# Moving layer 1's first layer norm and its first two turns into the last steps of layer 0's attention

## The chip, the cores and the metric

The kernel runs on one core of a Trainium2 chip. The metric is the device time of one execution in microseconds; 870.31 us is the median of three runs of the kernel before (868.54, 870.31 and 872.8). The profile is of another execution of the same kernel. TensorE (PE) does the matmuls and the transposes, VectorE (DVE), ScalarE (ACT) and GpSimd (POOL) the rest, and SyncE (SP) issues most DMAs. Each engine works through its own list of instructions in order; they are tied together by semaphores that count up.

## The reference, cut to what matters

Sixteen sequences of 256 tokens with 128 features pass two layers. Each layer normalises, and adds to x an attention and a mixture of experts of the normalised x.

```
xn = layernorm(x)                                    # (x - mean) / sqrt(var + 1e-5), by token
x  = x + softmax_attention_16_heads(xn) + top2_experts(xn)      # layer 0
xn = layernorm(x)                                    # the first step of layer 1
q, k, v = xn @ Wq, xn @ Wk, xn @ Wv;  gated = xn @ W1;  logits = xn @ Wr
x  = x + retention(q, k, v, gated) + top_p_experts(xn, logits)  # layer 1
```

The change is about the place where layer 0's attention of the last sequences ends and layer 1's projections begin. Layer 1's layer norm of a sequence can start when that sequence's x is complete: attention added, experts added.

## The kernel before, in words

Layer 0's attention works in 64 groups of four heads: group g belongs to sequence g // 4. All engines run through slots n = 0 to 67 (`run_groups`, with TAIL0 = 4 slots behind the last group). The order in each slot is written out by hand, as a function `slot` for each engine, and spreads a group over several slots. PE in slot n: the early scores of group n+3, in slots with n % 4 = 2 the turn of a finished sequence's heads (`turn_heads`), in slots with n % 4 = 3 its output projection (`attention_out`), the transposed scores of group n (`scores_t`), the turn of group n-2's output (`turn_out`), the late scores of n+3, the turn of the row maxima of n+2 (`turn_max`), and the weighting of the values of group n-1 (`weigh`). ACT: the copy of the turned heads in slots with n % 4 = 2 (`put_heads0`), the exponential of group n (L808), the negation of the row maxima of n+2 (`negate_max`, L782), the evacuation of n-1 (`evacuate`, L788). DVE: the second row maximum of n+2 (`row_max_second`, L1163), in slots with n % 4 = 3 the addition of a sequence's attention (`add_attention`, L1244), the division of n-2 (`divide`, L1234 and L1236), the first row maximum of n+3 (L1158), and statistics for layer 1's norm (`stats_of`). SP moves the negated maxima into the query stack (L464), from where `scores_t` two slots later reads them. POOL masks the exponentials of group n.

A sequence's attention is added four slots after its last group; the last sequence, 15, ends as slot 66 (turn of heads), slot 67 (output projection, addition, statistics).

Layer 1's norm takes the variances in two lots, EARLY for the first 24 tiles of 128 tokens (sequences 0 to 11) and LATE for the other eight. `variance_of(EARLY)` stands in DVE's slot 60, behind `divide` and the first row maximum. Behind all slots come, on ACT, the square root (`deviation1`, with a load of the function table), then, when `shift_of` on DVE has given reciprocal and shift, `normalise(0,0)`, `normalise(1,1)`, `high_x(0,0)`, `normalise(2,0)`, `high_x(1,1)`. `normalise` takes a sequence in two activations (L851) and `high_x` copies its turned form out of PSUM (L856); `low_x` on DVE (L1279) makes the rest for the two-part fp32 products. PE waits for all of layer 0's additions, then `transposes(0,0)` and `transposes(1,1)` (L1690), then for each of the sixteen sequences `products` (twelve matmuls, L1696) and `transposes` of the sequence two further on. This is what stands at PE's seam:

```
            run_groups(slot, middle, TAIL0)
            pe.wait_ge(x_attn, B)
...
            pe.wait_ge(consts_ready, 7)
            transposes(0, 0)
            transposes(1, 1)
```

PSUM banks 0 and 1, which take the turns, hold scores in layer 0; bank 7 and the upper half of bank 6 hold layer 0's turned output and heads, and later the second sequence's second product.

Of the kernel before, what the change touches and what calls it, by code (L numbers as in the profile page):

```python
# [13 lines left out]
ds = bass.ds  # L14
# [46 lines left out]
def build(nc, a, out):  # L61
    ctx = ExitStack()
    with ctx:
# [218 lines left out]
        def run_groups(slot, middle=None, tail=0):  # L282

            for n in range(G0 + tail):
                if n == MIDDLE * RING and middle is not None:
                    middle()
                slot((0, n))
# [77 lines left out]
        def ps_t1(u): return ps[:, u, 0:S]  # L365
# [373 lines left out]
        def _(act):  # L739
# [44 lines left out]
            def evacuate(g):  # L784
                act.wait_ge(pv_done, num(g) + 1)
                if past(g, 2):
                    act.wait_ge(o_turned, num(g) - 1)
                nc.scalar.activation(o_ring[:, at(g, 2), :], ps_o, ACT.Copy).then_inc(o_evac, 1)  # L788
# [12 lines left out]
            def slot(g):  # L801
                if g[1] % GPB0 == 2 and past(g, 6):
                    put_heads0(div(plus(g, -6), GPB0), 1 - g[1] // GPB0 % 2)
                if within(g, G0):
                    act.wait_ge(st_done, num(g) + 1)
                    if past(g, 2):
                        act.wait_ge(pv_done, num(g) - 1)
                    nc.scalar.activation(probs[:, at(g, 2), :, :], ps[:, 3:6, :], ACT.Exp, scale=float(D) ** -0.5)\  # L808
                      .then_inc(exp_done, 1)
                if within(plus(g, 2), G0):  # L810
                    negate_max(plus(g, 2))
                if past(g, 1) and within(plus(g, -1), G0):
                    evacuate(plus(g, -1))
                if num(g) == COUNT + 1:
                    act.wait_ge(pick_d, 1)
                    nc.scalar.activation(r_s[:, 1, 0, :], r_s[:, 0, 0, :], ACT.Exp).then_inc(pick_e, 1)
# [15 lines left out]
            def put_down(e):  # L832
# [1 line left out]
                for c in range(2 * e, 2 * e + 2):  # L834
                    last = nc.scalar.activation(y_sb[:, c, :], ps[:, 4 + e % 2, (c - 2 * e) * D:(c - 2 * e + 1) * D], ACT.Copy, scale=p_slot[:, c:c + 1])
                last.then_inc(y_put, 1)
            run_groups(slot, middle, TAIL0)

            def deviation1(n, tiles):
                act.wait_ge(var_ready, n)  # L840
                nc.scalar.activation(std[:, tiles], var[:, tiles], ACT.Sqrt).then_inc(std_ready, 1)
            deviation1(1, EARLY)


            def normalise(b, u):

# [7 lines left out]
            def high_x(b, v):  # L854
                act.wait_ge(tr_done, B + b + 1)
                nc.scalar.activation(r32(x_hl[:, 0, ds(b * S, S)]), ps_t1(v % 2), ACT.Copy).then_inc(xh_put, 1)  # L856

            def parts(b, v):
                u = v % 2
                act.wait_ge(p1_mm, b + 1 + CREDIT)  # L860
                nc.scalar.activation(sg[:, ds(b * TB, TB), :], p1_both(u)[:, :, D + E:PROJ1], ACT.Silu).then_inc(sg_put, 1)
                if isinstance(b, int) and b == 3:
                    deviation1(2, LATE)
                if more(b, 2):
                    high_x(b + 2, (v + 2) % 4)
                if more(b, 3):
                    act.wait_ge(tr_done, B + b + 2)
                    normalise(b + 3, 1 - u)
            act.wait_ge(rstd_ready, 2 * B + 2)
            act.wait_ge(wo_mm, B)  # L870
            normalise(0, 0)
            normalise(1, 1)
            high_x(0, 0)
            normalise(2, 0)
            high_x(1, 1)

            def step1(b, v):
                parts(b, v)
# [92 lines left out]
        def _(dve):  # L971
# [212 lines left out]
            def slot(g):  # L1184
                n = num(g)
                if within(plus(g, 2), G0) and n != MIDDLE * RING:
                    row_max_second(plus(g, 2))
                if n == COUNT:
                    take_counts()
                if n == FIND + 1:  # L1190
                    index_out()
                if n % GPB0 == 3 and n >= 7:
                    add_attention(div(plus(g, -7), GPB0))
                if n >= 2 and within(plus(g, -2), G0):
                    divide(plus(g, -2))
                if within(plus(g, 3), G0):
                    row_max_first(plus(g, 3))
                if n == 0:
                    add_router_bias()
                    mark_best(0)  # L1200
                if n == 1:
                    pick_first(0)
                if n == 2:
                    mark_best(1)
                if n == 3:
                    pick_first(1)
                if n == COUNT + 1:
                    count_ahead()
                if n == COUNT + 2:
                    pick_places()  # L1210
                if n == COUNT + 3:
                    index_in()
                if n == COUNT + 4:
                    mark_tiles()
                    weigh_experts()
                for m in range(MARKS):
                    if MARK - 1 + m * (FIND - MARK + 1) // MARKS == n:
                        mark_rows(m)
                for b in range(B):
                    if pair_counted(b) == n:  # L1220
                        stats_of(b)
                if n == G0 - 4:
                    variance_of(EARLY)
                if n == G0 + 3:
                    variance_of(LATE)

            def divide(g):

# [37 lines left out]
            run_groups(slot, middle, TAIL0)  # L1266


            def shift_of(n, tiles):
                dve.wait_ge(std_ready, B + n)  # L1270
                nc.vector.reciprocal(rstd[:, tiles], std[:, tiles]).then_inc(rstd_ready, 1)
                dve.wait_ge(rstd_ready, 2 * B + 2 * n - 1)
                nc.vector.scalar_tensor_tensor(out=shift[:, tiles], in0=moments[:, tiles, 0], scalar=-1.0, in1=rstd[:, tiles],
                                               op0=ALU.mult, op1=ALU.mult).then_inc(rstd_ready, 1)
            shift_of(1, EARLY)

            def low_x(b, v):
                dve.wait_ge(xh_put, b + 1)
                nc.vector.tensor_tensor(r32(x_hl[:, 1, ds(b * S, S)]), ps_t1(v % 2), x_hl[:, 0, ds(b * S, S)], ALU.subtract).then_inc(xl_put, 1)  # L1279
            dve.wait_ge(wo_mm, B)  # L1280
            low_x(0, 0)
            low_x(1, 1)
            dve.wait_ge(late_in, 13 * 16)

            def parts(b, v):
# [164 lines left out]
        def _(pe):  # L1450
# [137 lines left out]
            def slot(g):  # L1588
# [23 lines left out]
                    find_slots()  # L1612
                if past(g, 1) and within(plus(g, -1), G0):
                    weigh(plus(g, -1))

            def find_slots():

                pe.wait_ge(rows_marked, MARKS)
                pe.wait_ge(tiles_known, 10)
                for n in range(2 * NT):  # L1620
                    last = nc.tensor.matmul(ps_slots, of_row[:, n, :], of_tile[:, n, :, :].rearrange("p u c -> p (u c)"),
                                            start=(n == 0), stop=(n == 2 * NT - 1), skip_group_check=True)
                last.then_inc(slots_mm, 1)
# [56 lines left out]
                    down(e)  # L1680
                pe.wait_ge(y_put, E)
            run_groups(slot, middle, TAIL0)
            pe.wait_ge(x_attn, B)


            def transposes(b, u):
                pe.wait_ge(xn_second, (b + 1) * TB)
                pe.wait_ge(xl_put, b + 1)
                for t in range(TB):
                    last = nc.tensor.transpose(ps_t1(u)[:, t * P:(t + 1) * P], xn1_ring[:, u, t, :], ident[:, :])  # L1690
                last.then_inc(tr_done, 1)

            def three(dst, lhs, rhs):

                for k, (i, j) in enumerate(((0, 0), (1, 0), (0, 1))):
                    last = nc.tensor.matmul(dst, r32(lhs[i]), r32(rhs[j]), start=(k == 0), stop=(k == 2))  # L1696
                return last

            def products(b, v):
                u = v % 2  # L1700
                pe.wait_ge(xl_put, b + 1 + CREDIT)
                rhs = [x_hl[:, i, b * S:(b + 1) * S] for i in range(2)]
                pe.wait_ge(qk1_put, b + 1)
                for c in range(2):
                    last = three(ps_qk1(u)[:, c * S:(c + 1) * S], [w[:, c * P:(c + 1) * P] for w in w1_qk], rhs)
                last.then_inc(qk1_mm, 1)
                pe.wait_ge(lg1_put, b + 1)
                for t in range(TB):
                    last = three(ps_p1(u, t), [x_[:, t * P:(t + 1) * P] for x_ in rhs], [w[:, :] for w in w1_p])
                last.then_inc(p1_mm, 1)  # L1710
            pe.wait_ge(consts_ready, 7)
            transposes(0, 0)
            transposes(1, 1)

            def step(b, v):
                products(b, v)
# [225 lines left out]
```

## Time and profile before

| what | value |
|---|---|
| median of three runs | 870.31 us (868.54 to 872.8) |
| the profiled execution's own time | 864.98 us |
| its span, first to last instruction | 863.2 us |
| mean granted TensorE clock | 0.944 of full |
| PE busy | 755.5 us, 88% of the span |
| DVE, ACT, POOL busy | 556.3, 421.7, 311.3 us |
| share of PE in the chain that ended last | 70% |

Busy time is the union of an engine's instructions. The chain that ended last is followed back from the last instruction, at each step to what released it. Slot 61 begins at about 353.5 us of the span and the first products of layer 1 start at 376.01 us.

### The profile page before, as it was taken

How to read it: one execution, taken by the hardware profiler on the slowest of the kernel's cores; microseconds unless marked ns; L12 is line 12 of the kernel's file. 1: busy time of each engine (PE TensorE's matmuls, PEld its weight loads, DVE VectorE, ACT ScalarE, POOL GpSimd, SP SyncE). 2: the span in 40 equal slices, each digit the busy share in tenths (PEclk: the TensorE clock that was granted, in tenths of full speed). 3: DMA queues.
4: the chain of work that ended last, by engine and by line, in shares of the span. 5: the costliest groups of instructions: out<-in, count | busy, mean ns of one | idle time of the engine just before them, and what ended most of it. 6: DMA issues, size and time to landing. Idle time of an engine off the chain costs nothing.

```text
span 863.2 us, 17725 instructions
## 1 busy us (share of the span) xinstructions
PE 755.5 (88%) x6148; PEld 587.6 (68%) x6148; DVE 556.3 (64%) x1076; ACT 421.7 (49%) x788; POOL 311.3 (36%) x399
## 2 busy tenths in 40 slices
PE   4757889967978999768698879999999999999997
PEld 3644556745845666558576668888888888888886
DVE  4956799633534677547698757665656566666665
ACT  4723455534433656567666634444444444444442
POOL 1742357532032577500377736221211212121211
PEclk9977899988978999979899979999999999999999
DMA  5763465322012464100021137121111121211100
GB/s 174 223 198 118 134 196 201 93 73 79 8 53 74 133 180 134 51 2 1 27 64 51 50 92 147 39 67 42 61 48 61 49 61 49 61 49 61 49 13 12
DMA packets 58130, 70.71 MB, mean 82 GB/s; under 512 B 6608, under 2 KB 37840, under 8 KB 58064
## 3 DMA queue, kind: packets, MB, share of 16 engines
q1 hardware_dynamic: 56320, 67.46, 26.7%
q0 software_dynamic: 1024, 2.10, 0.8%
q8 instruction: 41, 0.67, 0.3%
q10 hardware_dynamic: 720, 0.27, 0.1%
q14 instruction: 25, 0.20, 0.1%
HBM read 53.80 MB, written 15.86 MB: 81 GB/s over the span
## 4 chain that ended last, share of the span: by engine, by line
PE 70%; DVE 10%; issue 6%; DMA 4%; ACT 3%; another core or an unknown queue 2%; POOL 2%; SPq 2%; ACTq 0%; DVEq 0%; POOLq 0%
PE ps L1696 23%; PE ps L1849 20%; PE ps L1562 3%; PE ps L1737 3%; PE ps L1545 3%; PE ps L1510 2%; DVE m L1163 2%; DMA q_st<-m_neg 2%; PE ps L1493 2%; PE ps L1663 1%; PE ps L1542 1%; PE ps L1628 1%; PE ps L1568 1%; PE ps L1497 1%
## 5 line engine op out<-in xcount | busy, mean ns | idle before, releaser
L1381 DVE SCALAR_TENSOR_TENSOR f_l<-ps,f_h 128x512 fp32r<-128x512 f32 x256 | 176.0, 691 | 114.1 <-ACT f_h L891 112.9
L891 ACT ACTIVATE f_h<-ps 128x512 fp32r<-128x512 f32 x256 | 153.3, 600 | 196.7 <-PE ps L1696 196.7
L1696 PE MATMUL ps<-x_hl,w_h 128*128 (+1 forms) x512 | 201.3, 393 | 0.0
L724 POOL TENSOR_TENSOR acc<-acc,yt 128x512 f32<-128x512 f32 x55 | 71.0, 1291 | 249.8 <-DVE yt L1419 249.8
L808 ACT ACTIVATE probs<-ps 128x1536 f32<-128x1536 f32 x64 | 92.9, 1452 | 78.6 <-PE ps L1545 71.0
L1696 PEld LDWEIGHTS ps<-x_hl,w_h 128*128 128x128 f32 x512 | 96.7, 189 | 19.7
L1849 PE MATMUL ps<-f_l,w_h 128*128 128x512 f32 x256 | 99.7, 390 | 0.6 <-DVE f_l L1381 0.6
L1696 PE MATMUL ps<-x_hl,w_l 128*128 (+1 forms) x256 | 100.1, 391 | 0.0
L1849 PE MATMUL ps<-f_h,w_h 128*128 128x512 f32 x256 | 99.7, 390 | 0.0
L1849 PE MATMUL ps<-f_h,w_l 128*128 128x512 f32 x256 | 99.6, 389 | 0.0
L633 POOL TENSOR_SCALAR_AFFINE_SELECT probs<-probs 128x512 f32<-128x512 f32 x96 | 63.6, 686 | 98.0 <-ACT probs L808 97.7
L1163 DVE TENSOR_REDUCE m<-ps 128x4 f32<-128x1024 f32 x64 | 77.8, 1216 | 5.0 <-PE ps L1510 4.8
L1234 DVE RECIPROCAL rden<-ps 128x8 f32<-128x8 f32 x64 | 13.2, 206 | 83.5 <-PE ps L1628 62.4
L1849 PEld LDWEIGHTS ps<-f_l,w_h 128*128 128x128 f32 x256 | 48.1, 188 | 11.1 <-DVE f_l L1381 1.1
L1696 PEld LDWEIGHTS ps<-x_hl,w_l 128*128 128x128 f32 x256 | 48.4, 189 | 9.5
L1849 PEld LDWEIGHTS ps<-f_h,w_l 128*128 128x128 f32 x256 | 48.1, 188 | 10.0
L1849 PEld LDWEIGHTS ps<-f_h,w_h 128*128 128x128 f32 x256 | 48.1, 188 | 10.0
L1562 PE MATMUL ps<-probs,v_ring 128*16 128x256 f32 x512 | 43.4, 413 | 8.2 <-DVE wv_tok L1236 8.2
L1158 DVE TENSOR_REDUCE m<-ps 128x4 f32<-128x512 f32 x64 | 43.6, 681 | 6.0 <-PE ps L1497 6.0
L788 ACT ACTIVATE o_ring<-ps 128x256 f32<-128x256 f32 x64 | 24.6, 385 | 43.5 <-PE ps L1568 26.4
L1330 DVE TENSOR_TENSOR sc<-ps,upto 128x1024 f32<-128x1024 f32 x32 | 37.8, 1219 | 8.5 <-PE ps L1737 7.8
L1510 PE MATMUL ps<-k_st,q_st 72*128 72x256 bf16 x256 | 42.7, 293 | 0.0
(226 smaller groups left out, 1427.3 us busy)
## 6 DMA issues: line engine op xcount, KB each, us to landing
gate_b<-gate_rows SPq DMA_DIRECT2D x64, 256.0 KB, 3.3
k_st<-qk_parts SPq DMA_DIRECT2D x32, 288.0 KB
q_st<-qk_parts SPq DMA_DIRECT2D x96, 96.0 KB
qk_parts<-qk_p SPq DMA_DIRECT2D x16, 384.0 KB, 2.8
y_tok<-zero SPq DMA_DIRECT2D x8, 512.0 KB, 3.3
w_raw<-in_w_e SPq DMA_DIRECT2D x16, 256.0 KB, 2.8
x_rows<-xn_ring SPq DMA_DIRECT2D x16, 128.0 KB, 2.6
w_up<-in_w_up SPq DMA_DIRECT2D x8, 256.0 KB, 2.9
```

Of the source, the lines that this page charges most:

```text
L633: nc.gpsimd.affine_select(tiles, tiles, pattern=[[0, GH], [1, P]], compare_op=ALU.is_ge, fill=0.0, base=0, channel_multiplier=-1)\
L724: nc.gpsimd.tensor_tensor(acc[:, :], acc[:, :], yt[:, e % 2, :], ALU.add).then_inc(summed, 1)
L808: nc.scalar.activation(probs[:, at(g, 2), :, :], ps[:, 3:6, :], ACT.Exp, scale=float(D) ** -0.5)\
L891: nc.scalar.activation(r32(f_h[:, m % 4, :]), ps[:, m % 4, :], ACT.Relu).then_inc(f_hi, 1)
L1158: nc.vector.tensor_reduce(m8[:, at(g, 2), :, 0], ps[:, first, :].rearrange("p (h k) -> p h k", h=GH), AX.X, ALU.max).then_inc(early_max, 1)
L1163: nc.vector.tensor_reduce(m8[:, at(g, 2), :, 1], ps[:, first + 1:first + 3, :].rearrange("p c (h k) -> p (c h) k", h=2), AX.X, ALU.max).th ...
L1330: nc.vector.tensor_tensor(sc[:, i % 3, :, 0:2 * P].rearrange("p h (j t) -> p h j t", t=P), diagonal(i % 2), upto[:, :].unsqueeze(1).unsque ...
L1381: nc.vector.scalar_tensor_tensor(out=r32(f_l[:, m % 4, :]), in0=ps[:, m % 4, :], scalar=0.0, in1=f_h[:, m % 4, :], op0=ALU.max, op1=ALU.su ...
L1510: last = nc.tensor.matmul(dst(1 + h // 2)[:, h % 2 * S:(h % 2 + 1) * S], qs[0:R0, h, P:S], ks[0:R0, h, :], start=False, stop=True, skip_gr ...
L1562: nc.tensor.matmul(ps_o[32 * h:32 * h + 2 * HD0, :], v_ring[:, u, 0, k * GH + h, :], probs[:, at(g, 2), 1 + h // 2, h % 2 * S:(h % 2 + 1) ...
L1696: last = nc.tensor.matmul(dst, r32(lhs[i]), r32(rhs[j]), start=(k == 0), stop=(k == 2))
L1849: last = nc.tensor.matmul(ps[:, 4 + e % 2, :], r32(w[i]), r32(fs[:, m % 4, :]), start=(c == 0 and k == 0), stop=(c == FC - 1 and k == 2))
```

## The change

In the slots of all three engines new steps are put in for the last groups (G0 is 64). EARLY's variances move from DVE's slot 60 to slot 62. The square root goes into ACT's slot 63, reciprocal and shift into DVE's slot 64, `normalise(0,0)` into ACT's slot 64, the first turn into PE's slot 65, and `normalise(1,1)`, `high_x(0,0)`, `normalise(2,0)`, `high_x(1,1)` into ACT's slot 66; `low_x(0,0)` into DVE's slot 66, `low_x(1,1)` into slot 67, the second turn into PE's slot 66. The waits in front of layer 1 on ACT (`wo_mm`), DVE (`wo_mm`) and PE (`x_attn`) go; PE's comes back ahead of the second sequence's second product, and PE gets three waits for the banks that the first steps take over. The bodies of the moved functions are otherwise the same.

```diff
@@ ScalarE, slot
+                if num(g) == G0 - 1:
+                    deviation1(1, EARLY)
+                if num(g) == G0:
+                    act.wait_ge(rstd_ready, 2 * B + 2)
+                    normalise(0, 0)
+                if num(g) == G0 + 2:
+                    normalise(1, 1)
+                    high_x(0, 0)
+                    normalise(2, 0)
+                    high_x(1, 1)
@@ ScalarE, behind the slots
-            deviation1(1, EARLY)
...
-            act.wait_ge(rstd_ready, 2 * B + 2)
-            act.wait_ge(wo_mm, B)
-            normalise(0, 0)
-            normalise(1, 1)
-            high_x(0, 0)
-            normalise(2, 0)
-            high_x(1, 1)
@@ VectorE, slot
-                if n == G0 - 4:
+                if n == G0 - 2:
                     variance_of(EARLY)
+                if n == G0:
+                    shift_of(1, EARLY)
+                if n == G0 + 2:
+                    low_x(0, 0)
                 if n == G0 + 3:
                     variance_of(LATE)
+                    low_x(1, 1)
@@ VectorE, behind the slots
-            shift_of(1, EARLY)
...
-            dve.wait_ge(wo_mm, B)
-            low_x(0, 0)
-            low_x(1, 1)
@@ TensorE, slot
+                if num(g) == G0 + 1:
+                    pe.wait_ge(max_done, G0)
+                    transposes(0, 0)
+                if num(g) == G0 + 2:
+                    transposes(1, 1)
+                if num(g) == G0 + 3:
+                    pe.wait_ge(consts_ready, 7)
+                    pe.wait_ge(exp_done, G0)
@@ TensorE, products
                 pe.wait_ge(lg1_put, b + 1)
+                if b == 1:
+                    pe.wait_ge(x_attn, B)
@@ TensorE, behind the slots
-            pe.wait_ge(x_attn, B)
...
-            pe.wait_ge(consts_ready, 7)
-            transposes(0, 0)
-            transposes(1, 1)
```

## Rows read from the trace of the kernel before

**Rows 1.** Chain that ended last, 340 to 400 us: start, duration, what.
```profile
342.91 0.56 PE ps L1562 x8
...
343.68 0.32 PE ps L1493
344.00 0.23 PE ps L1497 x4
...
345.38 0.22 PE ps L1628 x2
...
353.54 1.60 DVE moments L1173 x24
...
356.99 0.97 PE ps L1562 x8
...
360.29 0.42 PE ps L1628 x2
...
376.01 2.97 PE ps L1696 x12
...
383.58 1.46 PE ps L1696 x12
```

**Rows 2.** Timeline of DVE, slots 60 and 61: start, duration, operation, idle before.
```profile
353.45 1.68 DVE L1173 BATCH_NORM_AGGREGATE moments<-stats 128x2 f32<-128x6 f32 x24
...
355.25 1.22 DVE L1163 TENSOR_REDUCE m<-ps 128x4 f32<-128x1024 f32 x1
```

**Rows 3.** Timeline of PE, slot 61 to the first turns of layer 1.
```profile
356.53 0.27 PE L1524 MATMUL ps<-ident,m 128*8 128x128 f32 x1 [1.96 <-DVE m L1163]
...
361.34 0.62 PE L1562 MATMUL ps<-probs,v_ring 128*16 128x256 f32 x8 [0.65 <-DVE wv_tok L1236]
...
368.13 0.44 PE L1628 MATMUL ps<-ident,o_ring 128*128 128x128 f32 x2 [0.50 <-ACT o_ring L788]
369.17 0.41 PE L1636 MATMUL ps<-ident,wv_tok 128*128 128x128 f32 x2 [0.61 <-issue]
370.14 0.68 PE L1642 MATMUL ps<-w_o,wvn 128*128 128x128 f32 x4 [0.56 <-ACT wvn L794]
374.35 1.26 PE L1690 MATMUL ps<-ident,xn_ring 128*128 128x128 f32 x4 [3.52 <-ACT xn_ring L851]
```

**Rows 4.** Timeline of ACT, slot 61 to the first normalised sequences.
```profile
354.39 1.45 ACT L808 ACTIVATE probs<-ps 128x1536 f32<-128x1536 f32 x1 [0.35 <-PE ps L1545]
...
365.26 0.39 ACT L788 ACTIVATE o_ring<-ps 128x256 f32<-128x256 f32 x1 [0.28 <-PE ps L1568]
367.69 0.39 ACT L788 ACTIVATE o_ring<-ps 128x256 f32<-128x256 f32 x1 [2.04 <-PE ps L1568]
369.62 0.39 ACT L794 ACTIVATE wvn<-ps 128x256 f32<-128x256 f32 x1 [1.54 <-PE ps L1636]
370.02 1.28 ACT L841 ACT_TABLE_LOAD   x1
371.31 0.22 ACT L841 ACTIVATE std<-var 128x24 f32<-128x24 f32 x1
373.22 1.66 ACT L851 ACTIVATE xn_ring<-x,shift,rstd 128x128 f32<-128x128 f32 x4 [1.68 <-DVE shift L1273]
375.05 0.39 ACT L856 ACTIVATE x_hl<-ps 128x256 fp32r<-128x256 f32 x1 [0.17 <-PE ps L1690]
```

**Rows 5.** Timeline of DVE, shift and first rest of layer 1.
```profile
372.67 0.29 DVE L1271 RECIPROCAL rstd<-std 128x24 f32<-128x24 f32 x1
...
375.53 0.42 DVE L1279 TENSOR_TENSOR x_hl<-ps,x_hl 128x256 fp32r<-128x256 f32 x1 [2.35 <-ACT x_hl L856]
```

**Rows 6.** Chain that ended last over the whole span: one move of row maxima.
```profile
329.12 2.43 DMA q_st<-m_neg
```

**Rows 7.** Stretches of 1 us: busy us (count) by engine, granted clock, DMA share, GB/s.
```profile
357.00:358.00 1.00, 1.00 (x16) 0.54 (x16) 0.00 (x0) 0.10 (x1) 0.13 (x1) 0.56 0.08 16
...
381.00:382.00 1.00, 1.00 (x10) 1.00 (x10) 0.42 (x1) 0.34 (x2) 0.00 (x0) 0.99 0.08 16
```

More of the change, by code:

```diff
@@ L836, in put_down @@
                 last.then_inc(y_put, 1)
-            run_groups(slot, middle, TAIL0)
             def deviation1(n, tiles):
@@ L856, in high_x @@
                 nc.scalar.activation(r32(x_hl[:, 0, ds(b * S, S)]), ps_t1(v % 2), ACT.Copy).then_inc(xh_put, 1)
+            run_groups(slot, middle, TAIL0)
             def parts(b, v):
@@ L1221, in slot, with shift_of, low_x @@
                         stats_of(b)
-                if n == G0 - 4:
+                if n == G0 - 2:
                     variance_of(EARLY)
+                if n == G0:
+                    shift_of(1, EARLY)
+                if n == G0 + 2:
+                    low_x(0, 0)
                 if n == G0 + 3:
                     variance_of(LATE)
+                    low_x(1, 1)
+            def shift_of(n, tiles):
+                dve.wait_ge(std_ready, B + n)
+                nc.vector.reciprocal(rstd[:, tiles], std[:, tiles]).then_inc(rstd_ready, 1)
+                dve.wait_ge(rstd_ready, 2 * B + 2 * n - 1)
+                nc.vector.scalar_tensor_tensor(out=shift[:, tiles], in0=moments[:, tiles, 0], scalar=-1.0, in1=rstd[:, tiles],
+                                               op0=ALU.mult, op1=ALU.mult).then_inc(rstd_ready, 1)
+            def low_x(b, v):
+                dve.wait_ge(xh_put, b + 1)
+                nc.vector.tensor_tensor(r32(x_hl[:, 1, ds(b * S, S)]), ps_t1(v % 2), x_hl[:, 0, ds(b * S, S)], ALU.subtract).then_inc(xl_put, 1)
             def divide(g):
@@ L1266, in _ @@
             run_groups(slot, middle, TAIL0)
[L1269 to L1274, printed above, removed]
-            shift_of(1, EARLY)
-            def low_x(b, v):
-                dve.wait_ge(xh_put, b + 1)
-                nc.vector.tensor_tensor(r32(x_hl[:, 1, ds(b * S, S)]), ps_t1(v % 2), x_hl[:, 0, ds(b * S, S)], ALU.subtract).then_inc(xl_put, 1)
-            dve.wait_ge(wo_mm, B)
-            low_x(0, 0)
-            low_x(1, 1)
             dve.wait_ge(late_in, 13 * 16)
@@ L1614, in slot, with transposes, three, products @@
                     weigh(plus(g, -1))
+                if num(g) == G0 + 1:
[6 more added lines that the diff above has]
+                    pe.wait_ge(exp_done, G0)
+            def transposes(b, u):
+                pe.wait_ge(xn_second, (b + 1) * TB)
+                pe.wait_ge(xl_put, b + 1)
+                for t in range(TB):
+                    last = nc.tensor.transpose(ps_t1(u)[:, t * P:(t + 1) * P], xn1_ring[:, u, t, :], ident[:, :])
+                last.then_inc(tr_done, 1)
+            def three(dst, lhs, rhs):
+                for k, (i, j) in enumerate(((0, 0), (1, 0), (0, 1))):
+                    last = nc.tensor.matmul(dst, r32(lhs[i]), r32(rhs[j]), start=(k == 0), stop=(k == 2))
+                return last
+            def products(b, v):
+                u = v % 2
+                pe.wait_ge(xl_put, b + 1 + CREDIT)
+                rhs = [x_hl[:, i, b * S:(b + 1) * S] for i in range(2)]
+                pe.wait_ge(qk1_put, b + 1)
+                for c in range(2):
+                    last = three(ps_qk1(u)[:, c * S:(c + 1) * S], [w[:, c * P:(c + 1) * P] for w in w1_qk], rhs)
+                last.then_inc(qk1_mm, 1)
+                pe.wait_ge(lg1_put, b + 1)
+                if b == 1:
+                    pe.wait_ge(x_attn, B)
+                for t in range(TB):
+                    last = three(ps_p1(u, t), [x_[:, t * P:(t + 1) * P] for x_ in rhs], [w[:, :] for w in w1_p])
+                last.then_inc(p1_mm, 1)
             def find_slots():
@@ L1682, in _ @@
             run_groups(slot, middle, TAIL0)
-            pe.wait_ge(x_attn, B)
[L1686 to L1710, printed above, removed]
-            pe.wait_ge(consts_ready, 7)
-            transposes(0, 0)
-            transposes(1, 1)
             def step(b, v):
```

## The prediction

> **What bounds the kernel now.** I read the chain that ended last first, cut to 340 to 400 us, the stretch of the change. PE holds it nearly everywhere; the reader is to see the pieces that are not PE. One is DVE's aggregation for EARLY, 1.60 us of the chain at 353.54 [rows 1]. Then the timelines of single engines give the reason. In slot 60 DVE takes the 24 aggregations and one small operation from 353.45 to 355.25, 1.80 us, and only then the last group's second row maximum [rows 2]; PE, which has nothing left but to turn these maxima, idles 1.96 us for it [rows 3]. The second hole is at the seam: after the last output projection (370.14) PE does nothing for 3.52 us until ACT has normalised [rows 3]; ACT loads a table (1.28 us) and takes a root (0.22) from 370.02, waits 1.68 for DVE's shift, and needs 0.83 for each sequence [rows 4]. Last, the granted clock in stretches of 1 us: it falls from full to half between 357 and 358 us, just after the first hole, and the first products of layer 1 run at half as well, to 381 us [rows 7]: the first twelve matmuls take 2.97 us, twelve later ones 1.46 [rows 1]. So both holes are on the path that sets the end, and each is followed by half-clock work. From 383 us on the projections are a train of matmuls, so what is gained ahead of them is kept.
>
> All sums are against the profiled execution, 864.98 us (span 863.2 and 1.8 around it). That is 5.3 us below the median of the three runs, 870.31; I subtract the gain from that median, since nothing ties the difference to the stretch of the change.
>
> **Part 1, the variances go from slot 60 to slot 62.** Removed ahead of the row maximum: 355.25 - 353.45 = 1.80 us [rows 2]. The maximum then ends at 353.45 + 1.22 = 354.67, PE turns it at once, and with the division behind it on DVE (about 0.45) the weighting of group 60 starts near 355.15 instead of 356.99: 1.84 earlier. That closes the 1.96 us hole to some 0.3, and I expect no fall of the clock there. From that weighting to the end of the turn that feeds the next division there are six PE groups: 356.99 to 360.29 + 0.42, 3.72 us at half clock. The same six a few slots earlier take 342.91 to 345.38 + 0.22, 2.69, less 0.32 + 0.23 for two score groups that the last slots no longer have: 2.14 [rows 1]. Difference 1.58. What is late next: the turn of sequence 14's heads also waits for the negated maxima, which stand on ACT behind group 61's exponential, 354.39 + 1.45 = 355.84 [rows 4], and 0.27 more: 356.1, where the shortened work would be there at 355.9. That costs 0.2. Sum: 1.84 + 1.58 - 0.2 = **3.2 us**; the weighting of group 61 starts at 358.1, not 361.34 [rows 3]. If the clock falls all the same, the 1.58 goes and 1.6 is left; that is the low end.
>
> The negated maxima go through SP's queue; a move took 2.43 us from its issue to its landing where the chain ran through one [rows 6], so the last lands at 356.1 + 2.45 = 358.6, and the scores that read it come behind a weighting and an output projection, near 359.4. Covered by 0.8. SP has nothing ahead of it in these slots, and layer 1's first loads, next in its queue, come earlier too.
>
> The 1.80 us of variances now stand in slot 62 behind the division and ahead of the addition of sequence 14. Until DVE's next division is due PE must weight group 61 (0.62 and as much again), project (0.68) [rows 3], do group 63's scores (about 0.7) and turn (0.4): some 2.8 us against 1.80 + 0.42 for the addition. Cost nothing; with no such cover it would be the whole 1.80, the high end of its cost.
>
> **Part 2, the seam**, reckoned on the clock times of before and then shifted by part 1. ACT's copy of group 62's output ends at 365.65; load and root, 1.50, end at 367.15, and group 63's copy is not due before 367.69 [rows 4]. So 1.50 us of ACT are hidden, 0.54 to spare. DVE's reciprocal and shift, 372.67 to 373.2, 0.5 us [rows 4, 5], are then done at 367.7, while DVE is free.
>
> Here the Trainium skill, "ScalarE: Activation LUTs", section "What ACT_TABLE_LOAD costs", speaks against the change: a switch costs the load of about 1283 ns and a drain of about 1380 ns, 2.66 us in all. The trace agrees on the load and shows no drain: it starts 0.01 us after the copy ahead of it and the root 0.01 after it [rows 4]. By the page, group 63's copy would be 0.8 us late and the sum below 5.7 instead of 6.5.
>
> The steps from there: group 63's copy ends at 368.08; `normalise(0,0)`, half of 1.66, to 368.9; PE starts some 0.25 after its release, so the first turn runs 369.2 to 369.65. Behind it the turn of heads is late: 369.65 instead of 369.17, to 370.05 [rows 3]. ACT copies it (0.39) to 370.5, then `normalise(1,1)` to 371.35. PE's second turn waits for that, 371.6 to 372.05, and the last output projection, which was at 370.14, queues behind the turn: 372.05 to 372.65. So the added wait costs sequence 15's attention about 1.9 us; who waits for it is DVE's addition, and through it only the second sequence's second product. The first products need the rest of x: `high_x(0,0)` (0.39) to 371.75, `low_x(0,0)` (0.42) [rows 4, 5] to 372.2, earlier than PE is free. They start at 372.7, not 376.01 [rows 1]: **3.3 us**. Next in line is `low_x(1,1)`, behind addition, statistics and LATE's variances on DVE: 372.65 + 0.42 + 0.5 + 0.8 + 0.42, 374.9. With the first products at half clock (372.7 + 2.97 + turn = 376.1) it is hidden; at full clock PE would be there at 374.5 and wait 0.4 to 0.5.
>
> **The clock behind it** is the cost that no row gives. From group 62's weighting to the first products PE has about 8.3 us with short groups, busy some half of them, and the trace shows a fall of the clock after just such work. Low end of the gain: it falls ahead of the seam; then five short PE groups take 0.2 us more each, 1.0 in all. High end: it stays full, the first two products give back 1.5 each, less the 0.5 of waiting and another 1.0 of ACT and DVE that fall in behind, so 1.5. I take nothing, nearest to before, where two sequences' products ran at half.
>
> Sum: 3.2 + 3.3 = 6.5 us; 870.31 - 6.5 = **863.8 us** (the profiled execution 858.5).
>
> **The cases.**
> *Forecast, 863.8 us, chance 0.47*: both holes shorten, clock low for part of the time as before; its own range 862.5 to 865.5.
> *Clock stays full through the seam, 862.3 us, 0.20*: 6.5 + 1.5 = 8.0. For it: the two holes before the falls are nearly gone. Against: PE stays half idle for 8 us.
> *The first gain is small, 866.4 us, 0.22*: the clock still falls near 357 us (1.6 left of 3.2) and falls ahead of the seam (3.3 - 1.0), 3.9 in all. For it: what ended the stay at full clock was not the one hole alone; PE had been waiting off and on before the second fall. Against: PE is nearly dense up to 358 us now.
> *The change does not do what it says, 869 us, 0.06*: the waits only move. PE's turns block the last projection, ACT's load makes group 63 late, and the seam gives 0 to 1 us in place of 3.3, while part 1 gives its 1.6 less the variances' 1.80 showing up in slot 62. Against: the covers of 0.54, 0.8 and 0.6 us worked out above.
> *Slower, 876 us, 0.05*: the clock stays at half in the projections. Each sequence costs 2.97 - 1.46 = 1.5 us more at half [rows 1]. It decides from the fifth additional sequence on (5 x 1.5 = 7.5 against 6.5); with eight it is 12.0 - 6.5 = 5.5 slower. For it: the products start after a longer sparse stretch without a dense one. Against: in the trace a dense run brings the clock back, at 381 us, five after its start [rows 7].
>
> A measurement of this kernel can tell about 0.5%, 4.35 us, from no change: faster means below 865.96. That holds all of the first two cases but a twentieth, and a third of the third: 0.73; same 0.22; slower 0.05. The range of 8 in 10 runs from 860.6 to 867.4: it takes in the full clock, most of the third case, and the spread of 4 us among the runs of before.
>
> **What would show it.** In the changed kernel's trace: the wait of PE's turn of the maxima (L1524, its last) at 0.1 us or so, not 1.96; a granted clock of 1.00 from 354 to 360; no gap on DVE's side of more than 0.1 us ahead of group 62's weighting; the table load directly behind the second-last copy of outputs, and the last copy not later after its weighting than 0.1 us; PE's first products 6.5 us earlier, at 369.5, directly behind the last output projection; the second sequence's products not waiting more than 0.5. It is wrong if the table load shows a tail, if the last scores wait for the move of the maxima, if PE waits for DVE's division in slot 63, or if the clock stays at half beyond the third sequence.

## The result and the profile after

Six runs of the changed kernel gave 859.18 us in the median (855.65 to 860.35), six of the kernel before 870.09 (867.76 to 873.77): ratio 0.9869, interval 0.9836 to 0.9902, which is 11.4 us faster (8.5 to 14.3); the two medians differ by 10.9. I had forecast 863.8 with a range from 860.6: right in direction, too small in size, and outside the range by 1.4 us. The profiled execution took 856.11 us, 8.9 less than the one of before, with a span of 853.1, 10.1 less.

From the page of the changed kernel: span, busy PE, and the granted clock in 40 slices of the span (9 is 0.9 or more).

```profile
span 853.1 us, 17724 instructions
...
PE 754.8 (88%) x6148; PEld 585.8 (69%) x6148; DVE 556.3 (65%) x1076; ACT 420.5 (49%) x788; POOL 311.1 (36%) x399
...
PEclk9977899988978999999799879999999999999999
```

PE does the same work in the same busy time. What changed is where it stood still. The timeline of PE in the changed kernel, from the last turn of maxima to the first products (start, duration, operation, idle before); it answers to [rows 3]:

```profile
354.24 0.27 PE L1528 MATMUL ps<-ident,m 128*8 128x128 f32 x1
354.74 0.62 PE L1566 MATMUL ps<-probs,v_ring 128*16 128x256 f32 x8 [0.23 <-DVE wv_tok L1253]
...
357.53 0.62 PE L1566 MATMUL ps<-probs,v_ring 128*16 128x256 f32 x8 [0.65 <-DVE wv_tok L1253]
...
359.51 0.38 PE L1667 MATMUL ps<-ident,o_ring 128*128 128x128 f32 x2
360.55 0.63 PE L1566 MATMUL ps<-probs,v_ring 128*16 128x256 f32 x8 [0.65 <-DVE wv_tok L1253]
...
364.31 0.44 PE L1667 MATMUL ps<-ident,o_ring 128*128 128x128 f32 x2 [0.49 <-ACT o_ring L788]
365.12 0.41 PE L1632 MATMUL ps<-ident,xn_ring 128*128 128x128 f32 x2 [0.37 <-issue]
365.37 0.40 PE L1675 MATMUL ps<-ident,wv_tok 128*128 128x128 f32 x2
367.00 0.44 PE L1632 MATMUL ps<-ident,xn_ring 128*128 128x128 f32 x2 [1.24 <-ACT xn_ring L857]
367.27 0.61 PE L1681 MATMUL ps<-w_o,wvn 128*128 128x128 f32 x4
367.93 0.36 PE L1638 MATMUL ps<-x_hl,w_qk_hi 128*128 128x256 f32 x1
```

The idle 1.96 us ahead of the turn of maxima is gone, and of the 3.52 us in front of layer 1 there is left 1.24 in front of the second turn. The first products start at 367.93, not 376.01 [rows 1].

ACT in the changed kernel, slots 63 to 66, as [rows 4]:

```profile
361.45 0.38 ACT L788 ACTIVATE o_ring<-ps 128x256 f32<-128x256 f32 x1 [0.28 <-PE ps L1572]
361.85 1.28 ACT L849 ACT_TABLE_LOAD   x1
363.14 0.22 ACT L849 ACTIVATE std<-var 128x24 f32<-128x24 f32 x1
363.87 0.38 ACT L788 ACTIVATE o_ring<-ps 128x256 f32<-128x256 f32 x1 [0.51 <-PE ps L1572]
364.15 0.87 ACT L857 ACTIVATE xn_ring<-x,shift,rstd 128x128 f32<-128x128 f32 x2
365.80 0.38 ACT L794 ACTIVATE wvn<-ps 128x256 f32<-128x256 f32 x1 [0.78 <-PE ps L1675]
366.08 0.86 ACT L857 ACTIVATE xn_ring<-x,shift,rstd 128x128 f32<-128x128 f32 x2
```

The table load and the root stand in ACT's wait for group 63; 0.51 us of that wait is left over, where 0.54 had been reckoned. There is no tail behind the load: the root starts 1.29 us after the load does, as before.

DVE in the changed kernel, as [rows 2, 5]:

```profile
352.98 1.21 DVE L1164 TENSOR_REDUCE m<-ps 128x4 f32<-128x1024 f32 x1
...
357.30 1.68 DVE L1174 BATCH_NORM_AGGREGATE moments<-stats 128x2 f32<-128x6 f32 x24
...
359.38 0.41 DVE L1261 TENSOR_TENSOR x<-x,ps 128x256 f32<-128x256 f32 x1
359.93 0.21 DVE L1251 RECIPROCAL rden<-ps 128x8 f32<-128x8 f32 x1
...
369.72 0.42 DVE L1242 TENSOR_TENSOR x_hl<-ps,x_hl 128x256 fp32r<-128x256 f32 x1
```

The variances now run from 357.30, and with the addition behind them DVE is busy to 359.79. PE's turn, which the next division waits for, ends at 359.51 + 0.38 = 359.89. So they are hidden, but by 0.1 us, where the prediction had about 0.6: the steps on PE took 2.36 us, not 2.8.

The clock, in stretches of 6 us of the changed kernel (busy us and count by engine, granted clock, DMA share, GB/s), against the falls of [rows 7]:

```profile
356.00:362.00 6.00, 4.21 (x57) 2.87 (x55) 3.23 (x30) 4.23 (x7) 2.64 (x6) 1.00 0.66 173
362.00:368.00 6.00, 3.21 (x31) 1.90 (x31) 2.24 (x10) 4.70 (x12) 0.45 (x1) 1.00 0.01 4
368.00:374.00 6.00, 5.62 (x45) 5.33 (x46) 5.22 (x21) 4.79 (x12) 0.00 (x0) 1.00 0.02 4
```

It is full all the way, though PE is busy only half of the middle stretch.

### The profile page after: what moved, and what is told of

It is laid out like the page before. It is cut to its first block, busy times and chain, and to the rows that moved or that the text cites. A ratio compares the mean times of both kernels' runs of the same rounds, so it can differ in the third digit from the quotient of the medians.

```text
span 853.1 us, 17724 instructions
## 1 busy us (share of the span) xinstructions
PE 754.8 (88%) x6148; PEld 585.8 (69%) x6148; DVE 556.3 (65%) x1076; ACT 420.5 (49%) x788; POOL 311.1 (36%) x399
## 4 chain that ended last, share of the span: by engine, by line
PE 72%; DVE 10%; issue 5%; DMA 3%; ACT 3%; another core or an unknown queue 2%; POOL 2%; SPq 1%; ACTq 0%; DVEq 0%
PE ps L1638 22%; PE ps L1859 20%; PE ps L1566 3%; PE ps L1747 3%; PE ps L1549 2%; PE ps L1514 2%; DVE m L1164 2%; PE ps L1497 2%; PE ps L1702 1%; PE ps L1667 1%; PE ps L1546 1%; DMA q_st<-m_neg 1%; PE ps L1572 1%; PE ps L1501 1%
```

## Where the time went, stretch by stretch

To compare traces of different executions I cut each at the same instructions of PE. The columns, all worked out from starts in PE's timeline, in us: from the last group's early scores to group 60's weighting (the first hole lies in it), from there to group 61's, to group 63's, to the first products (the second hole), to the third sequence's products, to the seventh's, to the last product of the projections, and the sum. The kernel names are those of the experiments below.

```
kernel                        w60   w61   w63    p0    p2    p6   end    sum
before, first trace          6.22  4.35  5.45  9.22  5.59  9.47 17.25  57.55
before, second trace (r1)    6.22  4.28  5.45 10.49  4.95  9.47 17.19  58.05
changed, first trace         4.45  2.79  5.44  4.96  3.92  9.42 17.22  48.20
changed, second trace (r2)   4.45  2.78  5.44  5.08  4.54  9.41 17.22  48.92
e1 variances alone           4.44  2.79  5.45  9.73  4.84  9.46 17.21  53.92
e2 seam alone                6.22  4.46  8.31  6.36  5.36  9.45 17.22  57.38
e3 both holes filled         6.22  2.75  5.44  8.96  3.43  9.41 17.21  53.42
e6 first hole filled         6.22  2.75  5.44  9.72  4.84  9.46 17.22  55.65
e7 second hole filled        6.21  3.64  7.42 12.48  3.43  9.40 17.22  59.80
e4 second norm earlier       4.45  2.79  5.44  4.20  3.37  9.38 17.22  46.85
r3 the same again            4.45  2.78  5.44  4.20  3.35  9.40 17.22  46.84
e5 and LATE's root earlier   4.45  2.79  5.44  4.65  3.73  7.88 17.21  46.15
r4 the same again            4.45  2.79  5.44  4.19  3.28  7.91 17.21  45.27
e8 and gaps filled           4.45  2.79  5.44  4.19  3.30  7.89 17.21  45.27
```

For the first two traces the sum differs by 9.35 us: 1.77 in the first column (the wait for the maxima), 1.56 in the second (six PE groups at full clock), 4.27 up to the first products (5.45 + 9.22 against 5.44 + 4.96), 1.67 up to the third sequence (clock), 0.08 behind. The rest of the 10.1 us lies elsewhere: 0.48 ahead of slot 60 and 0.3 behind the projections, which the change does not touch.

## The experiments

They ran on other chips than the first comparison. There the kernel before takes 835 to 838 us; most of the 33 to 35 us less lies ahead of the stretch in question (its last early scores start at 318.32 us in the second trace, against 350.77). Ratios are therefore taken only against the kernel before on the same chip.

**e1, the variances alone.**

```diff
-                if n == G0 - 4:
+                if n == G0 - 2:
                     variance_of(EARLY)
```

> Only the variances move, from slot 60 to slot 62; the rest is the kernel before. Theory (the two parts add, and the clock follows the holes on PE): the last turn of maxima waits 0.1 us or less instead of 1.96, the clock stays full at 357 us, the weighting of group 61 starts some 3.3 us earlier, the seam is as before, its 3.5 us hole included, and so is the half clock behind it: 3.3 us faster in all, ratio near 0.996. Rival (part of the gain of the whole change hangs on both parts being there, or lies in how the clock falls elsewhere): the same seam, but a gain of 5 us or more, or of less than 2.

830.73 against 837.57 us, ratio 0.9924 (0.9895 to 0.9954), 6.4 us. That number is the rival's (5 us or more), and the theory's 3.3 lies below the interval, 3.8 to 8.8 us. The trace gives what the theory says: both columns of the first hole as in the changed kernel, the second hole as before, and half clock at the first products. From the chain that ended last of this kernel (start, duration, what):

```profile
337.92 0.68 PE ps L1690 x2
...
339.58 2.97 PE ps L1696 x12
```

The sum of stretches is 3.6 us shorter than in the first trace of before and 4.1 than in the second. So the mechanism in the trace is the theory's, and what the executions gain beyond it stays open.

**e2, the seam alone**: the changed kernel with the variances back in slot 60.

```diff
-                if n == G0 - 2:
+                if n == G0 - 4:
                     variance_of(EARLY)
```

> The changed kernel with the variances left in slot 60. Theory: hole of 1.96 us and half clock from 357 to 360 us as in the kernel before, then the seam 4.3 us shorter; if the clock holds through the seam as in the changed kernel, 1.7 us more: 6.0 in all, ratio near 0.993. Rival: the clock needs the first hole closed to stay full through the seam; then the first products of layer 1 run at half, each twelve in 2.97 us, and the gain is 4 us.

831.78 against 837.57, ratio 0.9927 (0.9895 to 0.9958), 6.1 us (3.5 to 8.8), which holds the theory's 6.0 and the rival's 4. Its trace is of the slowest of eight executions, 837.13 us, 5 above the median. There the first products run at half, as the rival says, and the half clock is much longer than either had it. Stretches of 6 us of this kernel,

```profile
326.00:332.00 6.00, 4.08 (x29) 2.39 (x29) 1.94 (x8) 2.46 (x5) 1.22 (x2) 0.65 0.17 51
332.00:338.00 6.00, 4.86 (x38) 3.16 (x42) 1.16 (x5) 2.73 (x3) 1.26 (x3) 0.50 0.38 127
338.00:344.00 6.00, 4.24 (x38) 1.68 (x30) 1.67 (x8) 3.03 (x6) 1.18 (x2) 0.50 0.01 1
344.00:350.00 6.00, 4.76 (x23) 4.33 (x22) 2.71 (x15) 3.73 (x8) 0.00 (x0) 0.50 0.01 1
350.00:356.00 6.00, 6.00 (x46) 5.90 (x44) 4.64 (x10) 4.45 (x13) 0.00 (x0) 0.86 0.01 3
```

The clock falls behind the first hole, at about 327.8 us, and stays at half to about 351.7. Groups 61 to 63 take 8.31 us instead of 5.45, the way to the first products 6.36 instead of 4.96, and in this execution the shorter seam is worth 0.2 us in the sum. So with the first hole open the seam's gain can be lost to the clock, as in this execution: the parts are not independent.

**e3, e6, e7, holes filled with idle matmuls, no wait changed.** Seven matmuls of 512 columns in front of the last turn of maxima, fifteen behind the last output projection; e3 has both, e6 the first, e7 the second.

```diff
+            def keep_busy(count):
+                pe.wait_ge(early_max, G0)
+                for _ in range(count):
+                    nc.tensor.matmul(ps[:, 0, :]..., ident_h[:, :], mask_qk[:, :]..., start=True, stop=True, ...)
...
+                if num(g) == G0 - 3:
+                    keep_busy(7)
                 if within(plus(g, 2), G0):
                     turn_max(plus(g, 2))
...
+            keep_busy(15)
             pe.wait_ge(x_attn, B)
```

> The kernel before with idle PE kept busy by matmuls whose result nobody reads: seven of 512 columns in front of the last turn of maxima, fifteen behind the last output projection, no wait changed. Theory (half clock follows from PE's holes and is worth 1.6 us behind the first and 1.7 to 2.6 behind the second): granted clock 1.00 from 350 to 385 us, first twelve products in 1.5 us instead of 2.97, gain 3.3 to 4.2 us with both waits still there. Rival (the clock falls for other reasons, or the projections are held by ACT and DVE at their start anyway): clock falls all the same, or it stays and the gain is below 1 us.

e3: 828.89 against 837.57, ratio 0.9915 (0.9882 to 0.9948), 7.1 us (4.4 to 9.9) for matmuls that nobody reads. In its trace both waits are there (first column 6.22, as before), the clock is full, and the first twelve products take 1.68 us. From the windows and the chain of e3:

```profile
336.00:342.00 6.00, 4.79 (x24) 2.31 (x23) 2.38 (x15) 4.23 (x10) 0.00 (x0) 1.00 0.01 3
```

```profile
342.20 1.68 PE ps L1706 x12
```

The sum is 4.1 us shorter than in the first trace of before, 4.6 than in the second, against the theory's 3.3 to 4.2. This isolates what the clock is worth: both waits are kept, and only the half clock is gone. The 7.1 us of the executions are more than the theory has, and its range lies below their interval.

> The kernel before with seven idle matmuls in the first hole only. Theory: the clock stays full at that place and through most of the last steps, and falls in the seam as in the first trace; gain 1.6 us against executions with a short half-clock period and 4 to 5 against those with a long one, 3 to 5 in the median. Rival (a filled hole is worth its own 1.6 us only): 1.6 in the median.

e6: 831.29 against 834.61, ratio 0.9970 (0.9942 to 0.9998), 2.5 us, between the theory's 3 and the rival's 1.6, so it does not tell them apart. Its trace gives 1.9 and 2.4 us against the two of before; the clock falls in the seam as there, the first products take it at half.

> The kernel before with fifteen idle matmuls behind the last output projection only; the first hole is as before. Theory (the half clock in the seam is a matter of the seam's own hole): it falls at the first hole and comes back, is full when the first products start, which take 1.7 us for twelve instead of 2.97; gain 2.2 us, as the difference between both holes filled and the first alone in the traces. Rival (the fall comes from the sparse steps ahead of the seam, not from the hole, and the filling comes too late): the first products run at half or nearly so, gain below 1 us.

e7: 834.84 against 835.37, ratio 0.9990 (0.9958 to 1.0022): nothing gained, the rival's number. Of its reasons one held: the clock fell at about 338.3 us, ahead of the filling. The other did not, for the first products ran at full clock. In its trace the clock fell at the first hole again and was low in most of what followed (7.42 us between groups 61 and 63), so the fifteen matmuls, made to fit 3.5 us at full clock, took longer than the hole. PE's timeline of e7:

```profile
342.43 1.20 PE L1649 MATMUL ps<-w_o,wvn 128*128 128x128 f32 x4 [0.56 <-ACT wvn L794]
343.42 5.93 PE L1592 MATMUL ps<-mask_qk,ident_h 128*128 128x512 bf16 x15
349.19 0.60 PE L1698 MATMUL ps<-ident,xn_ring 128*128 128x128 f32 x4
```

They held the first turns, which would have been ready 2.2 us earlier (3.52 us of hole against 5.77), while the products behind them came at full clock, 3.43 us for two sequences instead of 5.59. The two cancel.

**Which comes first in the seam, the hole or the fall.** The traces settle a point that the experiments above leave open. At the first hole the fall comes after it in each of the four traces that have it, 0.2 to 1.5 us after its end, and none of the ten others falls there. In the seam it is the other way round. From a window of 1 us and PE's timeline of the kernel before (r1, its second trace):

```profile
334.00:335.00 1.00, 0.73 (x16) 0.49 (x16) 0.52 (x3) 0.00 (x0) 0.00 (x0) 0.85 0.00 0
```

```profile
338.39 1.20 PE L1642 MATMUL ps<-w_o,wvn 128*128 128x128 f32 x4 [0.56 <-ACT wvn L794]
343.10 1.26 PE L1690 MATMUL ps<-ident,xn_ring 128*128 128x128 f32 x4 [3.52 <-ACT xn_ring L851]
```

The clock falls at about 334.7 us, and the hole begins at 339.58, 4.9 us later. In e1 and e6 the fall leads the hole by 1.7 us, and in the first trace of before it comes at 370.8, just when the hole begins. So the 3.5 us hole does not make the clock fall; it falls in the sparse steps ahead of it, where PE waits 0.5 to 0.65 us at a time. With the hole open the half clock then lasts 10.2 us (first trace, e1, e6) or 13.7 (r1) and runs into the products. Up to the end of the last output projection e3 and e6 do the same work on PE, and e6's clock falls there and e3's does not: that part of e3's full clock is the execution's, not the filling's. What decides whether it falls is not shown.

**r1 and r2, both kernels again**, unchanged.

> The kernel before, unchanged, for a second trace of it. Theory (the half clock that starts at the first hole is not always over in 3.4 us as in the first trace: the sparse steps behind it cannot bring it back, as in the trace of the seam part alone, where it lasted 24 us to the second products): in another execution the half clock covers the last steps and the seam, from group 60's weighting to the first products 21 us or more instead of 19.0, and the execution is longer by that. Rival (the first trace is typical): 19.0 again, within 0.3 us, and the same two short periods.

r1: 833.98 us in its profiled execution, ratio to the other runs of the same kernel 0.9995 (0.9961 to 1.0029). My theory fell, and so did the rival's 19.0: from group 60's weighting to the first products 20.2 us, not 21 or more, the half clock once more short at the first hole (second column 4.28, third 5.45) and falling earlier in the seam, where it costs 1.3 us before the products and gives 0.6 back behind. So the long period of e2 and e7 is not what every execution with the first hole has: two of four traces. In ten traces without that hole, groups 61 to 63 never took more than 5.45 us.

> The changed kernel, unchanged, on the same chip as its parts. Theory: the clock is full from the last steps of the attention to the projections' end again, 13.2 us from group 60's weighting to the first products; gain over the kernel before about 11 us, more than the 9.4 us that the first two traces give, since the kernel before loses more than its first trace shows. Rival: 9.4 us, the arithmetic of the two first traces.

r2: 825.19 against 834.61, ratio 0.9887 (0.9844 to 0.9929): 9.4 us (5.9 to 13.0), which is the rival's number, the arithmetic of two traces; the interval holds the theory's 11 as well. In its trace the clock was at half once, from about 332.0 to 335.4 us, at the first products (from 332.84), and cost 0.7 us in the sum. The theory's full clock failed there.

**e4 and r3, the second norm earlier.** What the changed kernel's trace shows as late next: ACT's `normalise(1,1)` behind the copy of the heads (PE idle 1.24 us), and `low_x(1,1)` behind LATE's variances (0.38).

```diff
-                if num(g) == G0 + 2:
+                if num(g) == G0 + 1:
                     normalise(1, 1)
+                if num(g) == G0 + 2:
                     high_x(0, 0)
...
-                    variance_of(LATE)
                     low_x(1, 1)
+                    variance_of(LATE)
```

> The changed kernel with normalise(1,1) in ACT's slot 65 instead of 66, and low_x(1,1) ahead of LATE's variances on DVE. Theory (what is late next in the seam is ACT's second norm, 1.24 us of PE idle, and DVE's variances, 0.38): the second turn follows the turn of heads with 0.3 us or less, the first products start 0.8 to 1.0 us earlier, the second ones do not wait: 1.0 to 1.4 us faster than the changed kernel, 10.5 faster than the one before. Rival: ACT is only filled earlier, the copy of the turned heads comes later by as much, and the output projection stays where it is: within 0.4 us of the changed kernel.

> The version with normalise(1,1) in slot 65 and low_x(1,1) ahead of LATE's variances once more, beside the two that build on it. Theory: 1.3 us faster than the changed kernel, so near 0.987 of the kernel before, and 1.4 us behind the version with LATE's root moved. Rival: level with it, since their ratios in two different jobs were both 0.985.

Ratios 0.9852 (0.9817 to 0.9887) and 0.9891 (0.9847 to 0.9934) against the kernel before. The two traces agree with each other to the hundredth and with the theory's 1.3: 1.35 us less than the changed kernel's first, 0.76 ahead of the first products and 0.55 behind. PE's timeline of e4:

```profile
334.83 0.40 PE L1676 MATMUL ps<-ident,wv_tok 128*128 128x128 f32 x2
335.31 0.44 PE L1633 MATMUL ps<-ident,xn_ring 128*128 128x128 f32 x2
335.80 0.68 PE L1682 MATMUL ps<-w_o,wvn 128*128 128x128 f32 x4
336.64 0.35 PE L1639 MATMUL ps<-x_hl,w_qk_hi 128*128 128x256 f32 x1 [0.16 <-issue]
```

The second turn follows the turn of heads, and the copy of the heads is not late. In the medians 1.35 us cannot be told: r3's ratio is level with the changed kernel's 0.9887 in r2.

**e5 and r4, LATE's root ahead of the first Silu** as well.

```diff
+                first = isinstance(b, int) and b == 0
+                if first:                              # ScalarE
+                    act.wait_ge(tr_done, B + b + 2)
+                    normalise(b + 3, 1 - u)
+                    high_x(b + 2, (v + 2) % 4)
+                    deviation1(2, LATE)
                 act.wait_ge(p1_mm, b + 1 + CREDIT)
                 ... ACT.Silu ...
-                if isinstance(b, int) and b == 3:
-                    deviation1(2, LATE)
...
+                if first:                              # VectorE, ahead of the wait for sg_put
+                    low_x(b + 2, (v + 2) % 4)
+                    shift_of(2, LATE)
```

The warming Silu behind the fourth sequence goes too.

> The second version of the seam (normalise(1,1) in slot 65, low_x(1,1) ahead of LATE's variances) and LATE's root taken ahead of the first Silu, while the root's table is still loaded, with the fourth sequence's norm and the third's copy in front of it; the warming Silu and two of three table loads go. Theory (the loads behind the fourth sequence cost PE two waits of 2.7 us together in every trace): these waits go, the first Silu comes 0.5 to 1.5 us later, of which PE sees 0.5 or less: 2.2 to 2.7 us faster than that version without it. Rival (the loads only fill time in which ACT is ahead, or the later Silu holds the first products' second half): within 1 us of it.

> The version with LATE's root ahead of the first Silu once more. Theory: from the first to the seventh sequence's products 11.6 us against 13.0 without it, 1.4 us and not 2.7, because the first Silu now holds the third sequence's second product: 1.4 us faster than the version without it in the same job. Rival: no difference beyond 0.5 us.

e5: 822.35 us beside r2's 825.19, ratio 0.9852 (0.9809 to 0.9894); r4: 822.54 beside r3's 826.73, ratio 0.9836 (0.9796 to 0.9876). r3 has two waits of PE for ACT's norms, behind the table loads; from its timeline:

```profile
348.78 0.44 PE L1633 MATMUL ps<-ident,xn_ring 128*128 128x128 f32 x2 [1.32 <-ACT xn_ring L858]
...
351.60 0.44 PE L1633 MATMUL ps<-ident,xn_ring 128*128 128x128 f32 x2 [0.97 <-ACT xn_ring L858]
```

In r4 they are gone, and one new one has come, for the first Silu's tail; from its timelines of ACT and PE:

```profile
339.58 0.20 ACT L850 ACTIVATE std<-var 128x8 f32<-128x8 f32 x1
339.80 1.28 ACT L876 ACT_TABLE_LOAD   x1
341.09 0.66 ACT L876 ACTIVATE sg<-ps 128x256 f32<-128x256 f32 x2
...
342.01 0.51 PE L1637 MATMUL ps<-w_p_hi,x_hl 128*128 128x264 f32 x2 [0.40 <-DVE v L1298]
```

Sum 45.27 against 46.84, 1.57 us (e5's 46.15 holds some half clock at the first products), as r4's theory has it and less than the 2.2 to 2.7 of e5's. This version beats both kernels in the median: 12 to 13 us under the kernel before, 2.8 under the changed one on the same chip, though their intervals overlap.

**e8, its gaps filled**: two idle matmuls in each of five waits of PE between group 62's weighting and the last projection.

```diff
+                if num(g) in (G0, G0 + 1):
+                    keep_busy(2)              # ahead of turn_out
...
+                if num(g) in (G0 - 1, G0):
+                    keep_busy(2)              # ahead of weigh
...
+                if num(g) == G0 + 3:
+                    keep_busy(2)              # ahead of attention_out
```

> The version with LATE's root moved, with ten idle matmuls of 512 columns, two in each of five waits of PE of 0.4 to 0.65 us between group 62's weighting and the last output projection. Theory (PE half idle there is what lets the clock fall now and then): clock full through the seam in the trace, 0.4 to 1.0 us faster than the version without them in the median. Rival (the matmuls stand in the way of the steps behind them, 0.22 us at a time): no faster, or slower by up to 0.5 us.

822.44 against r4's 822.54, and the same sum, 45.27: no gain, no harm. r4 had full clock there already, so the trace does not test whether they would have kept it.

## Why the prediction was right in kind and wrong in size

**Part 1** held. Reckoned 3.2 us, found 3.33: 1.77 for the wait (1.84 reckoned) and 1.56 for the six PE groups at full clock (1.58, less 0.2 for the negated maxima, which stood in the way less than thought). The variances in slot 62 cost nothing, and the last scores did not wait for the maxima's move.

**Part 2, the seam**, was mis-sized: 3.3 us reckoned, 4.27 found. The order of the steps was right, and so was the second turn queued ahead of the last projection. The sizes were not, because I laid durations end to end where the trace has the next instruction start before the one ahead has ended. ACT's `normalise(0,0)` starts 0.28 us after the start of a copy listed as 0.38; two transposes listed as 0.41 are followed by the next pair after 0.25; PE started the first turn 0.10 us after its release, not 0.25. With these the turn of heads is not late at all: 365.37 is 369.18 on the clock of before (3.81 us added), where it was 369.17. I had put it at 369.65. The trace is ahead of my sum by 0.47 us there, by 0.79 at the second turn (370.81 against 371.6) and by 0.96 at the first products (371.74 against 372.7).

**The clock behind it** is the step that failed: "I take nothing, nearest to before, where two sequences' products ran at half." The trace has full clock from 350 us to the projections' end, worth 1.67 us at the first two sequences, just above my high end of 1.5 for that term. e3 shows the size: with both waits left and the clock full, two sequences take 3.43 us instead of 5.59. I had priced the half clock as unchanged, although the change closes 2.3 of the 3.5 us between the last output projection and the products. My reading that each hole "is followed by half-clock work" hid the order: at the seam the fall comes before the hole or with it. Of the seven traces with the first hole closed and the seam shortened, five have full clock there and two (r2 and e5) about 3.4 us at half. The four with the seam's hole open and unfilled (before, r1, e1, e6) have 10.2 us or more. So a shorter stay at half, or none, is what goes with the change. That it comes from the dense products starting sooner fits the traces, but no run tests it alone, and the full clock of the first trace is in part luck. The case "Clock stays full through the seam", at 0.20, was what happened, with 8.0 us for what came to 9.35; 0.97 us of the seam, 0.17 of the clock and 0.13 of part 1 are most of the rest. Three small sums of the prediction are off, and nothing hangs on them: `low_x(1,1)` comes to 374.8, not 374.9, the case at 869 adds up to about 870, and the chance of 0.73 to 0.71.

**The range.** 9.35 us from the traces would have given 861.0, inside the range. The median was 859.18, 11.1 under the 870.31 that I started from, 1.8 more than the traces account for. On a second chip the same comparison gave 9.4, and the two intervals overlap widely, so some of the difference is the spread of executions, for which I had allowed too little at the low end. e2 and e7 suggest more: with the first hole open some executions lose another 2 to 3 us between groups 61 and 63, which no trace without the hole does. That would also fit e1's 6.4 and e3's 7.1 us, each above its own trace. The mean granted clock of all executions on e3's chip fits as well: 0.947 in the median for the kernel before and 0.964 for e3. My estimate from it, for 830 us of which each one at half clock counts half, is 28 us less at half, where the first trace has 13.6 in this stretch (3.4 and 10.2). Where in the span the rest lies is not shown: four traces with the hole, two long, do not say how often the kernel before has it, and neither trace of before does.

The slower case (clock at half through the projections) did not occur in any of fourteen traces. The waits did not merely move: each of the three covers held, the one in slot 62 by 0.1 us. On the Trainium skill's figure of 2.66 us for a switch of tables ("ScalarE: Activation LUTs", "What ACT_TABLE_LOAD costs"): the change put a load on the path's edge, and the copy behind it came when PE released it, 0.51 us after the root; with 1.38 us more it would have been late by 0.87. The measurement decides for 1.28.

## What to carry to other kernels

A wait that is taken away from a half-idle TensorE stretch can pay twice: its own length, and the half clock around it (here 1.77 and 1.56 us at the first hole). Price both. Look at the granted clock on each side of every hole: where the fall comes first, the hole is not its cause, and closing it may shorten the half clock without preventing it. When a chain of short operations is reckoned, take the spacing of starts from the trace, not the sum of durations; here that was 0.96 us of the seam's 4.3. And filling a hole with idle matmuls is a test of the clock, not a mend: sized at full clock, the filling overruns the hole when the clock is at half.

## What was not expected of the hardware

Half clock that begins at a hole of 1.96 us lasted 3.4 us in two traces (before, r1) and far longer in e2, from 327.8 to 351.7 us on another chip, with the same instructions up to the hole. In the seam of the kernels that keep the 3.5 us hole the clock fell as it began or up to 4.9 us before. Twenty-two matmuls whose result nobody reads made the kernel 7.1 us faster. And the order of work in ACT with two table loads less (r4) gained 1.57 us where the waits that went were 2.3: a later first Silu took a part back.
